# Cross-attention over 1601 keys: chunks of keys taken in pairs, with one value projection for two chunks

## The chip, the core and the metric

The kernel runs on one core of one Trainium2 chip. The metric is the device time of one execution in microseconds (us). Time before: 2998.97 us, the median of 3 runs (2998.92 to 2999.44).

The engines are named as in the profile: PE (TensorE, the matmuls), PEld (its weight loads), DVE (VectorE), ACT (ScalarE), POOL (GpSimd), SP (the queue that issues DMAs).

## What is computed

Six layers in a row on x, 16 x 64 x 256 (batch, queries, width), in fp32. The change touches the first and the fourth, two cross-attentions with 16 heads of 16 from the 64 queries to 1601 context rows:

```python
q = query @ Wq + bq;  k = key @ Wk + bk;  v = value @ Wv + bv      # per head: 64 x 16, 1601 x 16, 1601 x 16
attn = softmax((q @ k.T + relative) / sqrt(16))                    # layer 0: relative positions; layer 3: a mask of keys
x = x + (attn @ v (+ relative values)) @ Wo + bo
```

Between and after them stand a latent attention, a mixture of experts, a delta-rule layer and a gated MLP, which the change leaves alone.

## The kernel before

`cross_attention` (from L149) is called twice, once with `rel` (relative positions; "layer 0" below) and once with `mask` ("layer 1" below, the second cross-attention). It walks over the 16 batches b, two per loop turn (p = 0, 1). Each engine has a `body(bank, plan, i, p, flags)` with its own order of work, written out by hand, and engines meet only at semaphores. An engine takes its instructions strictly in this order.

One body does three things at once: it attends for batch b, prepares the keys and the score maxima of batch b + 1 ("ahead"), and finishes the output of batch b - 1 ("tail"). The first body (b = 0) has no tail and the last (b = 15) nothing ahead; the 14 between have all three.

The 1601 keys are 13 chunks (NCH) of 128, the last of 65. For each chunk c, PE does:

- the value projection: 2 matmuls of 256 columns on the whole 128 x 128 array, into bank `PJ[0]` (L726). As fp32 each is recorded as two. DVE copies the result from the bank into the buffer `V` (L537), which has 2 places;
- `scores(c)`: bf16 matmuls that subtract the row maximum (L688) and fp32 matmuls of q and k (L692), all on 32-row tiles of the array, four at a time, into banks 1 to 4. ACT takes the exponential of all four banks into a place of `PT` (L433); `scores(c + 1)` waits for it, since there is one set of score banks;
- `attend_values(c - 1)`: 16 matmuls of 64 columns (32 as recorded) on 32-column tiles of the array (L678), from V and PT, summed in bank 7.

Between these stand 16 units `maximum(u)`: bf16 scores of batch b + 1 for one of 4 key blocks and a quarter of the heads (L636, L640, in layer 0 also L645 for the first four units), into banks 5 and 6, on 32-row tiles. DVE reduces them (L525). There is one pair of banks for this, so `maximum(u)` on PE waits until DVE has read `maximum(u - 1)` (`max_read`). The tables EARLY and LATE (L278, L279) say after which chunk's value projection, or after which value product, a unit stands.

The tail of batch b - 1 also stands in this sequence: `denominators()` at c = 2 (L654: one matmul into bank 5, then on DVE a reciprocal and a product, L506 and L508) and `output()` at c = 5 (L663: the output projection into bank 6, then DVE adds it to X, L518). Banks 5 and 6 are those of the maxima, so both wait on the maxima already issued:

```python
if ahead:
    pe.wait_ge(max_read, UN * (b + 1) + U_DEN)     # U_DEN = 2: units 0 and 1 have been read
...
    pe.wait_ge(max_read, UN * (b + 1) + U_WO)      # U_WO = 6: units 0 to 5 have been read
```

In the order of before, unit 1 stands at the end of chunk 1, with chunk 2's projection, scores and a value product between it and `denominators()`; unit 5 stands after the projection of chunk 5, with the scores and a value product between it and `output()`. After the 13 chunks come, for batch b + 1, eight key projections (L584, 11 us), and at the start of the next body a transpose of the maxima (L721) that DVE turns into `nmb` (L530).

Of the kernel before, what the change touches and what calls it, by code (L numbers as in the profile page):

```python
# [13 lines left out]
B, S, D = 16, 64, 256  # L14
# [136 lines left out]
def cross_attention(nc, g, n, ctx_t, w, rel=None, mask=None):  # L151
# [5 lines left out]
    with nc.cleanup_on_exit(), ExitStack() as ctx:  # L157
        def sb(name, shape, dt=F32):
            return ctx.enter_context(nc.sbuf_tensor(tag + name, shape, dt))
# [22 lines left out]
        V = sb("V", [128, 2, H, 32])  # L182
        PT = sb("PT", [128, 3, H * S])
# [56 lines left out]
        class Schedule:  # L240
# [3 lines left out]
            def __init__(self, bank, ahead, attend, tail):  # L244
                self.D = bank.use(0) if rel and ahead else None
                self.K = [[bank.use(1 + gg) for gg in (0, 1)] for _ in range(NKB)] if ahead else None
                self.NM = bank.use(0) if attend else None
                self.V = [bank.use(0) for _ in range(NCH)] if attend else None
                self.DEN, self.WO = (bank.use(1), bank.use(2)) if tail else (None, None)
# [77 lines left out]
        def _(pool):  # L327
# [5 lines left out]
            def body(bank, plan, i, p, flags):  # L333
# [33 lines left out]
                if attend and rel:  # L367

                    pool.wait_ge(exp_done, NCH * b + 1)
                    if later(b):  # L370
                        pool.wait_ge(rv_done, b)
                    for j in range(RD):
                        pool.tensor_tensor(  # L373
                            Ej[:, j, :].rearrange("p (h q) -> p h q", h=H),
                            PT[:, 2, :].rearrange("p (h q) -> p h q", h=H),
                            kmask[:, j, None, :].to_broadcast([128, H, S]), ALU.mult).then_inc(e_done, 1)
# [7 lines left out]
        def _(act):  # L384
# [19 lines left out]
            def body(bank, plan, i, p, flags):  # L404
# [13 lines left out]
                if attend:  # L418
                    if mask:
                        act.wait_ge(kbs_done, b + 1)  # L420
                    for c in range(NCH):
                        slot = 2 if c == 0 else c % 2
# [26 lines left out]
        def _(dve):  # L449
# [23 lines left out]
            def body(bank, plan, i, p, flags):  # L473
# [58 lines left out]
                for c in range(NCH) if attend else ():  # L532
                    pb, use = plan.V[c]
# [5 lines left out]
                    if ahead and c in EARLY:  # L539
                        maximum(EARLY[c])  # L540
                    if ahead and c in LATE:
                        maximum(LATE[c])
# [27 lines left out]
        def _(pe):  # L570
# [38 lines left out]
            def body(bank, plan, i, p, flags):  # L609
# [56 lines left out]

                def attend_values(c):
                    pe.wait_ge(exp_done, NCH * b + c + 1)
                    pb, use = plan.V[c]
# [5 lines left out]
                    slot = 2 if c == 0 else c % 2  # L675
                    for h in range(H):
                        r = 32 * (h % 4)
                        last = pe.matmul(OT[r:r + 32, S * (h // 4):S * (h // 4) + S], V[0:CHK[c], c % 2, h, :],  # L678
# [38 lines left out]
                if attend:  # L717
# [5 lines left out]
                    for c in range(NCH):  # L723
                        pb = take(bank, plan.V[c])
                        for cc in range(KC):
                            last = pe.matmul(PJ[pb][0:CHK[c], 0:D], cT[:, p, cc, 128 * c:128 * c + CHK[c]],  # L726
                                             wv[:, cc, :], start=cc == 0, stop=cc == KC - 1)
                        last.then_inc(full[pb], 1)
                        if ahead and c in EARLY:
                            maximum(EARLY[c])  # L730
                        if c == 0:
                            pb, use = plan.NM
                            pe.wait_ge(free[pb], bank.value(pb, use))
                            if rel:
                                pe.wait_ge(dx_done, b + 1)
                        scores(c)
                        if c:
                            attend_values(c - 1)
                        if ahead and c in LATE:
                            maximum(LATE[c])  # L740
                        if tail and c == C_DEN:
                            denominators()
                        if tail and c == C_WO:
                            output()
# [1720 lines left out]
```

## Time and profile before

| | |
|---|---|
| median of 3 runs | 2998.97 us |
| the profiled execution's own time | 2999.0 us |
| its span, first to last instruction | 2996.8 us |
| PE busy | 2745.4 us (92%) |
| DVE busy | 1402.4 us (47%) |
| ACT busy | 1068.5 us (36%) |
| POOL busy | 478.0 us (16%) |
| mean granted TensorE clock, whole span | 0.963 of 2.4 GHz |

Times in the rows are microseconds from the start of the span unless marked ns. A matmul's record ends with a modelled tail, so busy sums of PE overlap; where a change of kind costs time is better read from the starts of the weight loads (PEld), which is how the rows below are used. In a timeline, neighbouring instructions of one kind are merged into a row with their count.

### The profile page before, as it was taken

To read this page: it belongs to the slowest core of one execution; us is meant where nothing else is said; L and a number is where in the kernel's file an instruction comes from. 1 tells how busy PE (TensorE), PEld (TensorE's weight loads), DVE (VectorE), ACT (ScalarE), POOL (GpSimd) and SP (SyncE) were. 2 spreads that over 40 slices of the span, in tenths; PEclk is the share of its full clock that TensorE was granted. 3 is DMA by queue.
4 is the path that set the end of the run, shared out by engine and by line. 5 is a ranking of instruction groups with operands and counts; after the bars stand their busy time and mean duration, and the time that the engine had idled before them with its cause. 6 is when DMAs were issued, how large, how long until landed. Compare 5 with 4: busy or idle time off the path is not lost. (4 is left out here: it accounts for less than half of the span.)

```text
span 2996.8 us, 95364 instructions
## 1 busy us (share of the span) xinstructions
PE 2745.4 (92%) x43444; PEld 1882.4 (63%) x43444; DVE 1402.4 (47%) x2425; ACT 1068.5 (36%) x1483; POOL 478.0 (16%) x406
## 2 busy tenths in 40 slices
PE   6999999999998789988999999999968999998798
PEld 3666666666666556655666666666646777777565
DVE  3443544544544821115454544545444555454378
ACT  2333333333332321123434344343434444444323
POOL 2424334234232000001000000000001112111000
PEclk8999999999998689999999999999979999999899
DMA  2110110111100011030111111111020000000100
GB/s 85 30 41 24 35 35 24 35 35 30 35 8 13 1 43 42 28 122 18 29 41 29 35 35 30 40 27 38 8 78 3 3 3 3 3 3 4 75 1 15
DMA packets 48631, 88.97 MB, mean 30 GB/s; under 512 B 8496, under 2 KB 43120, under 8 KB 46832
## 3 DMA queue, kind: packets, MB, share of 16 engines
q1 hardware_dynamic: 48240, 82.96, 9.1%
q8 instruction: 343, 5.62, 0.8%
q14 instruction: 48, 0.39, 0.0%
HBM read 81.89 MB, written 1.05 MB: 28 GB/s over the span
## 5 line engine op out<-in xcount | busy, mean ns | idle before, releaser
L525 DVE TENSOR_REDUCE x_mx<-banks 128x2 f32<-128x800 f32 (+1 forms) x512 | 506.9, 992 | 306.1 <-PE banks L640 217.0
L726 PE MATMUL banks<-x_wv,x_cT 128*128 128x256 f32 (+1 forms) x1664 | 465.9, 402 | 24.2 <-DVE x_nmb L530 21.1
L584 PE MATMUL banks<-x_cT,x_wk 128*128 128x400 f32 (+1 forms) x1024 | 362.9, 510 | 18.0 <-DMA x_cT<-in_ctx 18.0
L726 PEld LDWEIGHTS banks<-x_wv,x_cT 128*128 128x128 f32 (+1 forms) x1664 | 278.7, 186 | 145.4 <-issue 75.7
L433 ACT ACTIVATE x_PT<-banks 128x1024 f32<-128x1024 f32 (+1 forms) x208 | 212.8, 1023 | 430.0 <-PE banks L692 358.5
L433 ACT ACTIVATE x_PT<-banks,x_kbs 128x1024 f32<-128x1024 f32 (+1 forms) x208 | 231.5, 1113 | 376.7 <-PE banks L692 376.7
L584 PEld LDWEIGHTS banks<-x_cT,x_wk 128*128 128x128 f32 x1024 | 193.0, 192 | 163.6 <-issue 27.6
L692 PE MATMUL banks<-x_qbd,x_kT 32*128 32x128 f32 x6656 | 294.3, 273 | 0.0
L678 PE MATMUL banks<-x_PT,x_V 128*32 128x64 f32 x13312 | 272.1, 222 | 20.7 <-ACT x_PT L433 20.7
L692 PEld LDWEIGHTS banks<-x_qbd,x_kT 32*128 32x128 f32 x6656 | 253.2, 182 | 0.0
L678 PEld LDWEIGHTS banks<-x_PT,x_V 128*32 128x32 f32 x13312 | 204.9, 109 | 73.7 <-ACT x_PT L433 25.8
L389 ACT ACTIVATE x_kT<-banks,x_bk 128x400 f32<-128x400 f32 (+1 forms) x256 | 152.2, 595 | 255.2 <-PE banks L584 255.2
L365 POOL CAST x_kbf<-x_kT 128x800 bf16<-128x800 f32 (+1 forms) x128 | 110.3, 874 | 773.0 <-ACT x_kT L389 724.0
L537 DVE COPY x_V<-banks 128x256 f32<-128x256 f32 (+1 forms) x416 | 176.1, 423 | 122.5 <-PE banks L726 107.3
L640 PE MATMUL banks<-x_kbf,x_qbf 32*128 32x400 bf16 (+1 forms) x1024 | 173.1, 334 | 11.8 <-POOL x_kbf L365 7.4
L373 POOL TENSOR_TENSOR x_Ej<-x_PT,x_kmask 128x1024 f32<-128x1024 f32 x64 | 151.6, 2400 | 93.4 <-ACT x_PT L433 93.4
L530 DVE TENSOR_TENSOR x_nmb<-banks,x_pmask 128x256 bf16<-128x256 f32 x32 | 13.6, 424 | 308.2 <-PE banks L721 308.2
L688 PE MATMUL banks<-x_nmb,x_ones 32*128 32x256 bf16 (+1 forms) x1664 | 155.6, 277 | 1.8 <-ACT x_PT L433 1.8
L1840 PE MATMUL banks<-d_KQ,d_KB 64*64 64x64 f32 x3584 | 129.7, 221 | 8.2 <-ACT d_KB L1524 3.5
L1204 DVE SCALAR_TENSOR_TENSOR X<-banks,e_comb,X 128x256 f32<-128x256 f32 x72 | 34.8, 484 | 209.7 <-PE banks L1242 198.1
L1840 PEld LDWEIGHTS banks<-d_KQ,d_KB 64*64 64x64 f32 x3584 | 117.0, 133 | 22.1 <-issue 21.9
L1229 PE MATMUL banks<-XNT,e_wu 128*128 128x512 f32 x288 | 128.5, 600 | 0.4 <-DVE e_pr L1165 0.4
(321 smaller groups left out, 3776.3 us busy)
## 6 DMA issues: line engine op xcount, KB each, us to landing
x_cT<-in_ctx SPq DMA_DIRECT2D x96, 400.0 KB, 3.7
x_cT<-in_ctx SPq DMA_DIRECT2D x32, 401.0 KB, 3.6
e_wu<-in_mo_up SPq DMA_DIRECT2D x9, 512.0 KB, 3.6
e_wd<-in_mo_down SPq DMA_DIRECT2D x9, 512.0 KB, 4.4
x_mrow<-in_mask_row SPq DMA_DIRECT2D x1, 3202.0 KB, 11.1
t_w<-in_db_w SPq DMA_DIRECT2D x3, 1024.0 KB, 7.5
d_wqk<-in_db_qk SPq DMA_DIRECT2D x1, 2048.0 KB, 8.0
t_wgu<-in_fp_gu SPq DMA_DIRECT2D x1, 1536.0 KB, 10.4
```

The costliest lines, as they stand in the source:

```text
L373: pool.tensor_tensor(Ej[:, j, :].rearrange("p (h q) -> p h q", h=H), PT[:, 2, :].rearrange("p (h q) -> p h q", h=H), kmask[:, j, None, :]. ...
L389: act.activation(kT[:, 1 - p, gg, KB0[k]:KB0[k] + KBS[k]], PJ[pb][:, 0:KBS[k]], ACT.Identity, bias=bk[:, gg:gg + 1]).then_inc(free[pb], 1)
L433: act.activation(PT[0:CHK[c], slot, :].rearrange("p (r x) -> p r x", r=RT), g.PS[0:CHK[c], 1:1 + RT, 0:WS], ACT.Exp, scale=HD ** -0.5, bia ...
L525: dve.reduce_max(mx[:, H0[k]:H0[k] + 3:2, kb], g.PS[:, first:first + 2, 0:KBS[kb]], AXX).then_inc(max_read, 1)
L537: dve.tensor_copy(V[0:CHK[c], c % 2, :, 0:HD], PJ[pb][0:CHK[c], 0:D].rearrange("p (h d) -> p h d", h=H)).then_inc(free[pb], 1)
L584: last = pe.matmul(PJ[pb][:, 0:KBS[k]], wk[:, c, gg, :], cT[:, (p + 1) % 2, c, KB0[k]:KB0[k] + KBS[k]], start=c == 0, stop=c == KC - 1)
L640: last = pe.matmul(g.P[first + x][:, 0:KBS[kb]], qbf[rows(r), gg, :, :].rearrange("p i q -> p (i q)"), kbf[rows(r), gg, keys], start=not m ...
L678: last = pe.matmul(OT[r:r + 32, S * (h // 4):S * (h // 4) + S], V[0:CHK[c], c % 2, h, :], PT[0:CHK[c], slot, S * h:S * h + S], start=c == ...
L688: pe.matmul(SC[r][0:CHK[c], 0:WS], ones[rows(r), 0:CHK[c]], nmb[rows(r), :, :].rearrange("p j q -> p (j q)"), start=True, stop=False, skip ...
L692: last = pe.matmul(SC[r][0:CHK[c], HPT * S * gg:HPT * S * gg + HPT * S], kT[rows(r), p, gg, 128 * c:128 * c + CHK[c]], qbd[rows(r), p, gg, ...
L726: last = pe.matmul(PJ[pb][0:CHK[c], 0:D], cT[:, p, cc, 128 * c:128 * c + CHK[c]], wv[:, cc, :], start=cc == 0, stop=cc == KC - 1)
L1840: last = pe.matmul(out, lhs(E[e], hp), rhs(E[e], hp), start=k > 0 or start, stop=True, skip_group_check=True)
```

## The change

In both cross-attentions the chunks are walked in pairs. One value projection covers two chunks: 4 matmuls of 256 columns into the two halves of bank `PJ[0]`, one semaphore, and one DVE copy of 512 elements per partition. V gets 4 places instead of 2, PT 4 instead of 3. The order on PE for a pair (c, c + 1), c even, becomes: scores(c), a maximum (SCORED), projection of c + 2 and c + 3, a maximum (VALUED), scores(c + 1), attend_values(c - 1), a maximum (BETWEEN), attend_values(c). `denominators()` stands right behind the SCORED maximum of c = 2, which is unit 1, and `output()` right behind the VALUED maximum of c = 4, which is unit 5 (C_WO goes from 5 to 4). DVE's order follows. The waits inside `maximum`, `denominators` and `output` are unchanged. The diff, cut to its core:

```diff
-        V = sb("V", [128, 2, H, 32])
-        PT = sb("PT", [128, 3, H * S])
+        V = sb("V", [128, 4, H, 32])
+        PT = sb("PT", [128, 4, H * S])
...
-        EARLY = {4: 3, 5: 5, 6: 6, 8: 9, 10: 12, 12: 15}
-        LATE = {0: 0, 1: 1, 3: 2, 4: 4, 6: 7, 7: 8, 8: 10, 9: 11, 10: 13, 11: 14}
+        SCORED = {2: 1, 4: 4, 6: 7, 8: 10, 10: 13}
+        VALUED = {2: 2, 4: 5, 6: 8, 8: 11, 10: 14}
+        BETWEEN = {0: 0, 2: 3, 4: 6, 6: 9, 8: 12, 10: 15}
         C_DEN, U_DEN = 2, 2
-        C_WO, U_WO = 5, 6
+        C_WO, U_WO = 4, 6
...
-                        elif c >= 3:
-                            act.wait_ge(av_done, NCH * b + c - 1)
+                        elif c >= 4:
+                            act.wait_ge(av_done, NCH * b + c - 2)
...
+                def values(c):
+                    n2 = min(2, NCH - c)
+                    pb, use = plan.V[c // 2]
                     dve.wait_ge(full[pb], bank.value(pb, use))
-                    if later(b) or c >= 2:
-                        dve.wait_ge(av_done, NCH * b + (c - 1 if c >= 2 else 0))
-                    dve.tensor_copy(V[0:CHK[c], c % 2, :, 0:HD],
-                                    PJ[pb][0:CHK[c], 0:D].rearrange("p (h d) -> p h d", h=H)).then_inc(free[pb], 1)
+                    if later(b) or c >= 4:
+                        dve.wait_ge(av_done, NCH * b + (c - 2 if c >= 4 else 0))
+                    dve.tensor_copy(V[0:CHK[c], c % 4:c % 4 + n2, :, 0:HD],
+                                    PJ[pb][0:CHK[c], 0:D * n2].rearrange("p (a h d) -> p a h d", a=n2, h=H)).then_inc(free[pb], 1)
+                if attend:
+                    values(0)
+                for c in range(0, NCH, 2) if attend else ():
+                    if ahead and c in SCORED:
+                        maximum(SCORED[c])
                     if tail and c == C_DEN:
                         denominators()
+                    if ahead and c in VALUED:
+                        maximum(VALUED[c])
                     if tail and c == C_WO:
                         add_output()
+                    if c + 2 < NCH:
+                        values(c + 2)
+                    if ahead and c in BETWEEN:
+                        maximum(BETWEEN[c])
...
+                    project_values(0)
+                    for c in range(0, NCH, 2):
                         scores(c)
+                        if ahead and c in SCORED:
+                            maximum(SCORED[c])
+                        if tail and c == C_DEN:
+                            denominators()
+                        if c + 2 < NCH:
+                            project_values(c + 2)
+                        if ahead and c in VALUED:
+                            maximum(VALUED[c])
+                        if tail and c == C_WO:
+                            output()
+                        if c + 1 < NCH:
+                            scores(c + 1)
                         if c:
                             attend_values(c - 1)
+                        if ahead and c in BETWEEN:
+                            maximum(BETWEEN[c])
+                        if c + 1 < NCH:
+                            attend_values(c)
                     attend_values(NCH - 1)
```

## Rows read from the trace of the kernel before

**Rows 1.** Stretches inside layers 0 and 1: busy us (instructions) by engine, granted clock, DMA.

```profile
core 0: us, PE busy (x) PEld busy (x) DVE busy (x) ACT busy (x) POOL busy (x), PEclk, DMA share, GB/s
126.00:850.00 724.00, 705.59 (x11573) 472.43 (x11574) 333.77 (x497) 241.59 (x288) 250.72 (x171) 1.00 0.12 32
...
1430.00:2165.00 735.00, 711.28 (x11934) 458.60 (x11936) 356.44 (x520) 297.32 (x322) 47.06 (x55) 1.00 0.11 31
```

**Rows 2.** Waits of PE in the stretch 1430 to 2165 (layer 1).

```profile
PE banks L678 <- ACT x_PT L433: 9.7, 14, 0.7
PE banks L726 <- DVE x_nmb L530: 8.2, 15, 0.5
```

**Rows 3.** Timeline of weight loads: first projection of two neighbouring batches, layers 0 and 1.

```profile
291.35 0.73 PEld L726 LDWEIGHTS banks<-x_wv,x_cT 128*128 128x128 f32 x4 [0.82 <-DVE x_nmb L530]
...
346.52 0.73 PEld L726 LDWEIGHTS banks<-x_wv,x_cT 128*128 128x128 f32 x4 [0.81 <-DVE x_nmb L530]
...
1488.40 0.73 PEld L726 LDWEIGHTS banks<-x_wv,x_cT 128*128 128x128 f32 x4 [0.82 <-DVE x_nmb L530]
...
1540.63 0.73 PEld L726 LDWEIGHTS banks<-x_wv,x_cT 128*128 128x128 f32 x4 [0.81 <-DVE x_nmb L530]
```

**Rows 4.** Timeline of weight loads, layer 1, about chunks 8 and 9.

```profile
1512.61 0.73 PEld L726 LDWEIGHTS banks<-x_wv,x_cT 128*128 128x128 f32 x4 [0.33 <-issue]
1513.77 0.09 PEld L636 LDWEIGHTS banks<-x_mb,x_ones 32*128 32x128 bf16 x2 [0.43 <-DVE x_mx L525]
...
1514.77 0.49 PEld L678 LDWEIGHTS banks<-x_PT,x_V 128*32 128x32 f32 x32
1515.37 0.09 PEld L636 LDWEIGHTS banks<-x_mb,x_ones 32*128 32x128 bf16 x2
...
1515.82 0.73 PEld L726 LDWEIGHTS banks<-x_wv,x_cT 128*128 128x128 f32 x4 [0.33 <-issue]
1516.88 0.10 PEld L688 LDWEIGHTS banks<-x_nmb,x_ones 32*128 32x128 bf16 x4 [0.33 <-issue]
...
1517.55 0.49 PEld L678 LDWEIGHTS banks<-x_PT,x_V 128*32 128x32 f32 x32
```

**Rows 5.** Timeline of weight loads, layer 1: denominators, then the projection of chunk 3.

```profile
1495.54 0.30 PEld L654 LDWEIGHTS banks<-x_oT,x_selden 128*128 128x128 f32 x2
...
1497.03 0.10 PEld L688 LDWEIGHTS banks<-x_nmb,x_ones 32*128 32x128 bf16 x4 [0.33 <-issue]
```

**Rows 6.** Timeline of weight loads, layer 0: a maximum before scores, another before a projection.

```profile
318.31 0.09 PEld L640 LDWEIGHTS banks<-x_kbf,x_qbf 32*128 32x128 bf16 x2 [0.43 <-DVE x_mx L525]
...
319.14 0.49 PEld L678 LDWEIGHTS banks<-x_PT,x_V 128*32 128x32 f32 x32
319.75 0.09 PEld L640 LDWEIGHTS banks<-x_kbf,x_qbf 32*128 32x128 bf16 x2
320.02 0.73 PEld L726 LDWEIGHTS banks<-x_wv,x_cT 128*128 128x128 f32 x4 [0.18 <-issue]
```

**Rows 7.** Timeline of DVE: a reduction in layer 0, the reciprocal and a reduction in layer 1.

```profile
318.70 0.99 DVE L525 TENSOR_REDUCE x_mx<-banks 128x2 f32<-128x800 f32 x1
...
1496.28 1.76 DVE L506 RECIPROCAL x_rec<-banks 128x256 f32<-128x256 f32 x1 [1.46 <-PE banks L654]
...
1514.33 0.99 DVE L525 TENSOR_REDUCE x_mx<-banks 128x2 f32<-128x800 f32 x1
```

**Rows 8.** Groups by line and shape: busy us, mean ns of one | idle before.

```profile
L525 DVE TENSOR_REDUCE x_mx<-banks 128x2 f32<-128x800 f32 x384 | 379.8, 992 | 189.3 <-PE banks L640 183.1 <-issue 1.3
...
L433 ACT ACTIVATE x_PT<-banks,x_kbs 128x1024 f32<-128x1024 f32 x192 | 213.8, 1113 | 344.9 <-PE banks L692 344.9
L433 ACT ACTIVATE x_PT<-banks 128x1024 f32<-128x1024 f32 x192 | 196.5, 1023 | 401.9 <-PE banks L692 330.4 <-PE banks L699 71.5
...
L537 DVE COPY x_V<-banks 128x256 f32<-128x256 f32 x384 | 162.6, 423 | 118.5 <-PE banks L726 103.6
```

**Rows 9.** Timeline of ACT, layer 1: the exponential of the scores issued at 1516.88.

```profile
1517.75 1.11 ACT L433 ACTIVATE x_PT<-banks,x_kbs 128x1024 f32<-128x1024 f32 x1 [1.66 <-PE banks L692]
```

More of the change, by code:

```diff
@@ L247, in __init__ @@
                 self.NM = bank.use(0) if attend else None
-                self.V = [bank.use(0) for _ in range(NCH)] if attend else None
+                self.V = [bank.use(0) for _ in range(0, NCH, 2)] if attend else None
                 self.DEN, self.WO = (bank.use(1), bank.use(2)) if tail else (None, None)
@@ L421, in body @@
                     for c in range(NCH):
-                        slot = 2 if c == 0 else c % 2
+                        slot = 3 if c == 0 else c % 3
                         if c == 0:
@@ L531, in body @@
                                       pmask[:, :, None].to_broadcast([128, NPR, 128]), ALU.mult).then_inc(free[pb], 1)
-                for c in range(NCH) if attend else ():
-                    pb, use = plan.V[c]
+                def values(c):
+                    n2 = min(2, NCH - c)
+                    pb, use = plan.V[c // 2]
                     dve.wait_ge(full[pb], bank.value(pb, use))
-                    if later(b) or c >= 2:
-                        dve.wait_ge(av_done, NCH * b + (c - 1 if c >= 2 else 0))
-                    dve.tensor_copy(V[0:CHK[c], c % 2, :, 0:HD],
-                                    PJ[pb][0:CHK[c], 0:D].rearrange("p (h d) -> p h d", h=H)).then_inc(free[pb], 1)
[L539 to L542, printed above, removed]
+                    if later(b) or c >= 4:
[7 more added lines that the diff above has]
+                        maximum(SCORED[c])
                     if tail and c == C_DEN:
                         denominators()
+                    if ahead and c in VALUED:
+                        maximum(VALUED[c])
                     if tail and c == C_WO:
                         add_output()
+                    if c + 2 < NCH:
+                        values(c + 2)
+                    if ahead and c in BETWEEN:
+                        maximum(BETWEEN[c])
                 if ahead:
@@ L665, in output, with project_values @@
                     last.then_inc(full[pb], 1)
+                def project_values(c):
+                    pb = take(bank, plan.V[c // 2])
+                    for k in range(min(2, NCH - c)):
+                        for cc in range(KC):
+                            last = pe.matmul(PJ[pb][0:CHK[c + k], D * k:D * k + D], cT[:, p, cc, 128 * (c + k):128 * (c + k) + CHK[c + k]],
+                                             wv[:, cc, :], start=cc == 0, stop=cc == KC - 1)
+                    last.then_inc(full[pb], 1)
                 def attend_values(c):
                     pe.wait_ge(exp_done, NCH * b + c + 1)
-                    pb, use = plan.V[c]
+                    pb, use = plan.V[c // 2]
                     pe.wait_ge(free[pb], bank.value(pb, use))
@@ L674, in attend_values @@
                         pe.wait_ge(bias_out, 1)
-                    slot = 2 if c == 0 else c % 2
+                    slot = 3 if c == 0 else c % 3
                     for h in range(H):
                         r = 32 * (h % 4)
-                        last = pe.matmul(OT[r:r + 32, S * (h // 4):S * (h // 4) + S], V[0:CHK[c], c % 2, h, :],
+                        last = pe.matmul(OT[r:r + 32, S * (h // 4):S * (h // 4) + S], V[0:CHK[c], c % 4, h, :],
                                          PT[0:CHK[c], slot, S * h:S * h + S], start=c == 0 and h < 4,
@@ L722, in body @@
                     last.then_inc(full[pb], 1)
[L723 to L735, printed above, removed]
-                        scores(c)
+                    project_values(0)
+                    pb, use = plan.NM
+                    pe.wait_ge(free[pb], bank.value(pb, use))
+                    if rel:
+                        pe.wait_ge(dx_done, b + 1)
+                    for c in range(0, NCH, 2):
+                        scores(c)
+                        if ahead and c in SCORED:
[10 more added lines that the diff above has]
+                            scores(c + 1)
                         if c:
                             attend_values(c - 1)
[L739 to L744, printed above, removed]
+                        if ahead and c in BETWEEN:
+                            maximum(BETWEEN[c])
+                        if c + 1 < NCH:
+                            attend_values(c)
                     attend_values(NCH - 1)
```

2 lines of the change are left out of this document (1 added, 1 removed).

## The prediction

> **What bounds the kernel now.** I read first the busy table by stretch. Inside both cross-attentions PE is busy 97% of the time (705.59 of 724 us, 711.28 of 735) and no other engine half; the granted clock is 1.00 throughout, the 2.4 GHz level, and the DMAs are busy 12% [rows 1]. So only PE's sequence counts: what it issues, and what makes it wait. A batch takes 55.17 us in layer 0 and 52.23 us in layer 1, from one first projection to the next [rows 3]. PE's waits come to under 1.5 us of that [rows 2]; but those rows count idle time behind modelled matmul tails, and short waits vanish in them. So I went on to the starts of the weight loads. There every group of PE has a length from its first weight load to that of the next group [rows 4]: projection 1.06 us (1515.82 to 1516.88), scores 0.67 (to 1517.55), value product 0.60 (1514.77 to 1515.37; 0.58 in most places), maximum 0.45 (to 1515.82). In layer 0 a maximum is 0.27 (319.75 to 320.02) [rows 6].
>
> **What a change of kind costs.** Denominators and the projection behind them are both whole-array matmuls of 256 columns, six records together, and take 1.49 us [rows 5], against 1.06 for four: 0.215 per record, so four records cost 0.86 and the projection's entry and exit 0.20. A maximum of 0.45 and scores of 0.67 take 1.00 when they touch (1513.77 to 1514.77) [rows 4], 0.11 less; in layer 0 0.83 [rows 6]. These are what joining two groups of one kind saves. The trace shows no two projections side by side; the bounds are 0 and 0.20, and I take 0.20, the nearest row being the denominators with a projection.
>
> **What is removed.** The 13 projection groups become 7, six joins: 1.18 us a batch. In layer 0 chunk 2's projection also joins the relative-bias matmuls behind the first scores, 0.20 more. Maxima and scores touch more often (22 groups of 32-row kind become 19): 0.33. The value products join nothing: BETWEEN puts a maximum between the two of a pair, so "one run" is not what happens while a batch lies ahead. In layer 0 the first four maxima end in whole-array matmuls, which now meet a projection once instead of three times: 0.35 given back. Four of the new joins are spoiled by waits (below), 0.05 each. Net about -1.2 us in layer 0, -1.3 in layer 1. Waits also go. A maximum behind a projection waits 0.10 (1512.61 to 1513.77 is 1.16, not 1.06) [rows 4]; four such go, and with them the wait of chunk 4's projection for its bank, 0.2: -0.65 us.
>
> By the Trainium skill, TensorEngine Tiling (Key Properties), changing the tiling mode drains the engine. The trace agrees: 0.20 and 0.11 us per change in the joins above.
>
> **The cycle of a maximum.** Weights at 1513.77 [rows 4], reduction from 1514.33 for 0.99 [rows 7, 8], next maximum at 1515.37 [rows 4]: 1.60 us in layer 1. In layer 0 318.31, 318.70 [rows 6, 7], 319.75: 1.44. Nothing that waits on `max_read` can start sooner.
>
> **What is added: two long waits.** `denominators()` needs units 0 and 1 read, and now stands right behind unit 1. PE goes on 1.60 us after unit 1 began, of which 0.39 is the unit's own work: 1.2 us idle. In layer 0 the extra bias matmuls of units 0 to 3 lengthen both: 1.25. `output()` needs units 0 to 5 and stands right behind unit 5: again 1.2. Before, scores and a value product (1.25 us) lay between in the second case, more in the first; now nothing does, and everything later on PE is queued behind. Nothing hides them. That is 2.4 us a batch in both layers. Unit 2 must also wait until the reciprocal (1.76 us) [rows 7] has freed bank 5; it stands 0.54 + 1.92 us behind the start of the denominators: 0.2 more.
>
> **Shorter new waits.** (a) Scores(2) follow scores(1) with one maximum and one value product between. The exponential begins 0.87 us after its scores (1516.88 to 1517.75) [rows 4, 9], takes 1.11 or 1.02 [rows 8], and PE follows 0.06 later: 2.05 or 1.96 us. PE's own work there is 1.00 + 0.58 = 1.58 in layer 1: a wait of 0.47; in layer 0, with the bias matmuls, 0.22. For later pairs there are two value products between, 2.2 us and more: no wait. (b) The copy of V of two chunks. Reductions of 800 elements take 992 ns and copies of 256 take 423 [rows 8], so 1.046 ns an element: 0.69 us for 512. The bounds are 0.60 (the fixed part smaller) and 0.75. The copy waits for the value product just before the BETWEEN maximum, so it runs from 0.10 to 0.75 after that maximum's weights, its reduction from 0.78 to 1.77, and the SCORED maximum of the next pair cannot begin before 1.83. PE is there after 0.45 + 0.58 + 0.67 = 1.70 in layer 1 and 1.52 in layer 0: 0.13 and 0.31. In layer 0 this holds in three pairs (0.95), in layer 1 in four, one of them 0.18 (0.57); unit 1 is caught by (a) already, and unit 4 in layer 0 comes late enough. (c) In layer 1 chunk 2's projection waits 0.18 for the doubled copy of the first pair. The last wait of a batch, value product 12 for its exponential, stays.
>
> By the Trainium skill, VectorE: DVE Perf Modes (The TRN2 errata), a copy from PSUM costs 120 cycles plus one per element: 0.66 us for 512, an estimate. By it the result would be 4 us lower.
>
> **The sum.** Layer 0, per batch: 1.25 + 1.19 + 0.19 + 0.22 + 0.95 = 3.80, less 0.65 of waits and 1.2 of joins: +1.9. Layer 1: 1.19 + 1.19 + 0.19 + 0.47 + 0.57 + 0.18 = 3.79, less 0.65 and 1.3: +1.8. As a test of the method I laid out a whole batch, group by group and engine by engine, with these durations: the order of before comes out at 55.1 and 52.4 us, against 55.17 and 52.23 measured, and the new order at 57.0 and 54.2. 14 batches of each layer have everything: 14 x 3.7 = +51.8 us. The first batch has no denominators and no output, so only the gains and the small waits: -0.9 and -0.7. The last has no maxima; its value products do touch, but then scores wait for the exponential of the scores just before: -0.7 and +0.2. Together +49.7, rounded to 49. ACT, POOL and the loads of the context stay hidden (ACT has 1.6 us free per chunk, [rows 9]). Against the profiled execution's 2999.0 us (span 2996.8 and 2.2 around it), which equals the median of 2998.97, that gives 3048 us.
>
> **Rivals.**
>
> *The joins win* (faster). If every wait on `max_read` were covered, only joins and removed waits were left: -1.85 us in layer 0 and -1.95 in layer 1, times 14, and -2 for the edges, so about -55: 2944 us. For it speaks that PE takes weight loads ahead of running matmuls, so that a wait may cost less than the distance of starts suggests. It needs the waits cut by half to become faster: 3.8 us a batch would have to be under 1.9. Against it: the order in the code is plain, and the cycle of 1.60 us is seen at every second maximum, where PE does wait its 0.1. Taken alone, the Trainium skill's rule on draining (above) would give this case. Chance 0.07.
>
> *The two long waits are half as dear* (near no change). If the reduction of units 1 and 5 ran while something else of PE did, say because the tail's waits were met earlier than I read, 1.2 us a batch would go: 28 x 1.2 = 34 us less, 3014 us; with cheaper copies on top it could reach 3000. Chance 0.07.
>
> *Waits breed waits* (slower than forecast). DVE falls behind after the reciprocal and each maximum then finds its pair of banks late. Each further 0.3 us in five places a batch is 1.5 x 28 = 42 us: 3090. Against it: DVE is busy less than half of the time [rows 1], and the layout by engine already has its queue. Chance 0.08.
>
> *The clock.* The new waits of 1.2 us could drop the granted clock inside the stages. In [rows 1] it stays at 1.00 with the waits there are (0.8 at the start of each batch [rows 3]). If it fell to the 1.2 GHz level for a tenth of the 1510 us of both layers, that would cost some 75 us: 3120. Chance 0.03.
>
> **How the numbers follow.** The forecast, two waits of 1.2 us a batch and small ones, has 0.75. Its own range: the copy's bounds move the sum by -12 and +7, the joins (six a batch at 0.15 to 0.20) by up to +8, the small waits by -8 to +6: 3028 to 3066. Stretched to take in part of the milder and the dearer case: 3022 to 3068. A measurement of this kernel can tell about 0.2% (6 us) from no change. Faster than 2993: 0.08. Within: 0.03. Slower than 3005: 0.89.
>
> **What would show it.** In the profile after, DVE rows in the weight loads of L654 and L663 (in the new numbering) with some 1.2 us of idle time, 28 each; projections as eight records at 0.215 us each; V copies of 512 elements at 0.69 us; 57.0 and 54.2 us between first projections; granted clock 1.00. The forecast fails if PE shows no wait before the denominators and the output, or if two projections side by side take over 2.0 us, or if exponentials hold scores in every pair and not only at scores(2).

## The result

The changed kernel takes 3076.05 us, the median of 4 runs (3074.35 to 3078.87), against 2999.2 for the kernel before on the same chips: a ratio of 1.0253, 95% interval 1.0237 to 1.0268. It is 77 us slower. The forecast was 3048 us, 49 slower, with a range up to 3068: the direction was right, and a good third of the loss was missing.

The profile after, first the page's busy line and then the same two stretches as in [rows 1]:

```profile
PE 2715.8 (88%) x43444; PEld 1891.2 (62%) x43444; DVE 1392.9 (45%) x2233; ACT 1069.6 (35%) x1483; POOL 480.1 (16%) x406
```

```profile
126.00:850.00 724.00, 651.56 (x10856) 447.48 (x10854) 327.75 (x394) 226.74 (x269) 239.71 (x163) 1.00 0.11 30
1430.00:2165.00 735.00, 673.86 (x11453) 444.98 (x11454) 326.61 (x420) 286.36 (x309) 44.59 (x52) 1.00 0.12 32
```

PE is busy 90% and 92% of the stages instead of 97%, at the same granted clock of 1.00: it waits more. Time from one first projection to the next, as in [rows 3]:

```profile
359.99 1.59 PEld L681 LDWEIGHTS banks<-x_wv,x_cT 128*128 128x128 f32 x8 [0.82 <-DVE x_nmb L531]
...
418.60 1.59 PEld L681 LDWEIGHTS banks<-x_wv,x_cT 128*128 128x128 f32 x8 [0.81 <-DVE x_nmb L531]
```

```profile
1532.47 1.59 PEld L681 LDWEIGHTS banks<-x_wv,x_cT 128*128 128x128 f32 x8 [0.82 <-DVE x_nmb L531]
...
1586.76 1.59 PEld L681 LDWEIGHTS banks<-x_wv,x_cT 128*128 128x128 f32 x8 [0.81 <-DVE x_nmb L531]
```

That is 58.61 us a batch in layer 0 (before 55.17, forecast 57.0) and 54.29 in layer 1 (before 52.23, forecast 54.2). Times 14: 48 + 29 = 77 us. (The interval behind batch 14 is some 12 us shorter, since the key projections stand at the start of the next body, for the batch behind it, and the last body has none; it grows by the same 3.45 and 2.06 us.) Layer 1 is nearly as forecast; in layer 0 the forecast misses 1.6 us a batch.

The two long waits, in weight loads of layer 1 after, and then the reductions of units 1 and 5 on the vector engine:

```profile
1539.61 0.10 PEld L646 LDWEIGHTS banks<-x_mb,x_ones 32*128 32x128 bf16 x2
1539.72 0.10 PEld L650 LDWEIGHTS banks<-x_kbf,x_qbf 32*128 32x128 bf16 x2
1541.33 0.30 PEld L664 LDWEIGHTS banks<-x_oT,x_selden 128*128 128x128 f32 x2 [1.51 <-issue]
1541.66 1.70 PEld L681 LDWEIGHTS banks<-x_wv,x_cT 128*128 128x128 f32 x8
...
1549.78 0.09 PEld L646 LDWEIGHTS banks<-x_mb,x_ones 32*128 32x128 bf16 x2 [0.33 <-issue]
...
1551.40 1.49 PEld L673 LDWEIGHTS banks<-x_wo,x_oN 128*64 128x64 f32 x8 [1.51 <-issue]
```

```profile
1540.27 0.99 DVE L526 TENSOR_REDUCE x_mx<-banks 128x2 f32<-128x802 f32 x1 [0.99 <-PE banks L650]
...
1550.34 0.99 DVE L526 TENSOR_REDUCE x_mx<-banks 128x2 f32<-128x800 f32 x1 [1.38 <-PE banks L650]
```

From the weights of unit 1 to those of the denominators are 1.72 us, from those of unit 5 to those of the output projection 1.62, with a maximum of about 0.4 as the only work in between. Both follow the end of the reduction that the code makes them wait for by 0.07 us (1541.26 to 1541.33, 1551.33 to 1551.40). The profile puts the wait down to "issue" and not to the vector engine, where the forecast had looked for it.

And the place that the forecast did not see, layer 0 after. PE's loads, then the vector engine, then GpSimd, at the same time:

```profile
373.69 0.54 PEld L710 LDWEIGHTS banks<-x_qbd,x_kT 32*128 32x128 f32 x16
374.35 0.49 PEld L696 LDWEIGHTS banks<-x_PT,x_V 128*32 128x32 f32 x32
376.38 0.09 PEld L650 LDWEIGHTS banks<-x_kbf,x_qbf 32*128 32x128 bf16 x2 [1.54 <-DVE x_mx L526]
```

```profile
371.26 1.76 DVE L507 RECIPROCAL x_rec<-banks 128x256 f32<-128x256 f32 x1 [0.81 <-PE banks L664]
373.05 2.37 DVE L509 TENSOR_TENSOR x_oN<-x_oT,x_rec 128x256 f32<-128x256 f32 x1
375.35 0.98 DVE L526 TENSOR_REDUCE x_mx<-banks 128x2 f32<-128x802 f32 x1
```

```profile
365.86 9.28 POOL L374 TENSOR_TENSOR x_Ej<-x_PT,x_kmask 128x1024 f32<-128x1024 f32 x4 [5.13 <-ACT x_PT L434]
375.08 0.94 POOL L342 COPY x_qs<-x_qT 128x256 f32<-128x256 f32 x2
```

The product of 256 elements takes 2.37 us and ends just after GpSimd's four multiplications end (375.14). The reduction of unit 2 stands behind it on the vector engine, and PE waits 1.54 us for that before unit 3. In the kernel before, the same product took 0.48:

```profile
301.36 1.76 DVE L506 RECIPROCAL x_rec<-banks 128x256 f32<-128x256 f32 x1 [1.46 <-PE banks L654]
303.15 0.48 DVE L508 TENSOR_TENSOR x_oN<-x_oT,x_rec 128x256 f32<-128x256 f32 x1
```

```profile
296.36 9.48 POOL L373 TENSOR_TENSOR x_Ej<-x_PT,x_kmask 128x1024 f32<-128x1024 f32 x4 [4.27 <-ACT x_PT L433]
```

```profile
L373 POOL TENSOR_TENSOR x_Ej<-x_PT,x_kmask x4: 2358/2360/2542, 296.4 to 303.3; 128x1024 f32<-128x1024 f32 x4
```

(minimum, median and maximum in ns, then the first and the last start). It began at 303.15, just ahead of the start of the fourth of GpSimd's multiplications, at 303.3. That fourth one took 2.54 us there and the other three 2.36: here it was the product that came first. So the theory to test has three parts: two waits behind maxima, a product that GpSimd holds, and short waits that eat what the pairs save. Its rival: the rhythm of pairs itself is slow, and any wait taken away comes back at the next maximum.

### The profile page after: what moved, and what is told of

Same layout as the page of the kernel before. It is cut to its first block and busy times, and to the rows that moved or that the text cites. A ratio compares the mean times of both kernels' runs of the same rounds, so it can differ in the third digit from the quotient of the medians.

```text
span 3072.6 us, 94948 instructions
## 1 busy us (share of the span) xinstructions
PE 2715.8 (88%) x43444; PEld 1891.2 (62%) x43444; DVE 1392.9 (45%) x2233; ACT 1069.6 (35%) x1483; POOL 480.1 (16%) x406
## 5 line engine op out<-in xcount | busy, mean ns | idle before, releaser
L681 PE MATMUL banks<-x_wv,x_cT 128*128 128x256 f32 (+1 forms) x1664 | 417.5, 393 | 22.8 <-DVE x_nmb L531 21.1
L681 PEld LDWEIGHTS banks<-x_wv,x_cT 128*128 128x128 f32 (+1 forms) x1664 | 296.9, 188 | 104.2 <-issue 31.1
L710 PE MATMUL banks<-x_qbd,x_kT 32*128 32x128 f32 x6656 | 282.5, 271 | 0.0
L539 DVE COPY x_V<-banks 128x512 f32<-128x512 f32 (+1 forms) x224 | 146.0, 652 | 241.7 <-PE banks L681 163.0
L710 PEld LDWEIGHTS banks<-x_qbd,x_kT 32*128 32x128 f32 x6656 | 245.0, 182 | 0.0
L706 PE MATMUL banks<-x_nmb,x_ones 32*128 32x256 bf16 (+1 forms) x1664 | 143.6, 278 | 10.7 <-ACT x_PT L434 9.4
## 6 DMA issues: line engine op xcount, KB each, us to landing
x_mrow<-in_mask_row SPq DMA_DIRECT2D x1, 3202.0 KB, 11.1
```

What stands on the lines that cost most here:

```text
L539: dve.tensor_copy(V[0:CHK[c], c % 4:c % 4 + n2, :, 0:HD], PJ[pb][0:CHK[c], 0:D * n2].rearrange("p (a h d) -> p a h d", a=n2, h=H)).then_in ...
L681: last = pe.matmul(PJ[pb][0:CHK[c + k], D * k:D * k + D], cT[:, p, cc, 128 * (c + k):128 * (c + k) + CHK[c + k]], wv[:, cc, :], start=cc = ...
L706: pe.matmul(SC[r][0:CHK[c], 0:WS], ones[rows(r), 0:CHK[c]], nmb[rows(r), :, :].rearrange("p j q -> p (j q)"), start=True, stop=False, skip ...
L710: last = pe.matmul(SC[r][0:CHK[c], HPT * S * gg:HPT * S * gg + HPT * S], kT[rows(r), p, gg, 128 * c:128 * c + CHK[c]], qbd[rows(r), p, gg, ...
```

## The experiments

Each kernel is the changed one with one edit, unless said otherwise. "Batch" is the usual time between first projections, layer 0 / layer 1; ratios are to the kernel before on the same chip. A line `...` in a diff stands for lines left out.

**The output projection behind a value product.**

```diff
-                        if tail and c == C_WO:
-                            output()
                         if c + 1 < NCH:
                             scores(c + 1)
                         if c:
                             attend_values(c - 1)
+                        if tail and c == C_WO:
+                            output()
```

> The changed kernel with the output projection moved from right behind unit 5 to behind the value product of chunk 3, so that scores and a value product lie between unit 5 and it. Theory A (the wait behind unit 5 is a pure loss of about 1.2 us a batch in both layers): it goes, and unit 6, now right behind the output, waits 0.6 us for the addition to X; net -0.8 in both layers, 28 batches, 3076 - 23 = about 3053 us; 57.8 us a batch in layer 0 and 53.5 in layer 1. Theory B (the rhythm of the pairs sets the time and a wait taken away comes back at the next maximum): 3070 to 3080 us, batches still 58.6 and 54.3.

Measured: 3047.49 us, ratio 1.0159 (1.0142 to 1.0176); batch 57.58 / 53.38. The wait is gone and did not come back in full. What takes its place is the one that was expected, unit 6 behind the addition to X:

```profile
1541.03 1.49 PEld L673 LDWEIGHTS banks<-x_wo,x_oN 128*64 128x64 f32 x8
1543.48 0.09 PEld L646 LDWEIGHTS banks<-x_mb,x_ones 32*128 32x128 bf16 x2 [0.97 <-DVE X L519]
```

2.45 us for a group of 1.87: 0.6 waited. In all -29 us, a little more than the 23 expected. The batches of theory B, 58.6 and 54.3, are not seen: it falls for this wait.

**Units 0 and 1 one place earlier**, so that a value product and scores lie between unit 1 and the denominators.

```diff
-        SCORED = {2: 1, 4: 4, 6: 7, 8: 10, 10: 13}
+        SCORED = {0: 0, 4: 4, 6: 7, 8: 10, 10: 13}
-        BETWEEN = {0: 0, 2: 3, 4: 6, 6: 9, 8: 12, 10: 15}
+        BETWEEN = {0: 1, 2: 3, 4: 6, 6: 9, 8: 12, 10: 15}
```

> The changed kernel with unit 0 behind the scores of chunk 0 and unit 1 in unit 0's old place, so that a value product and scores lie between unit 1 and the denominators. Theory A: the 1.2 us wait before the denominators goes in both layers. In layer 0 the product behind the reciprocal starts earlier, at another point of GpSimd's four multiplications, and if it is those that hold it (2.37 us instead of 0.48) it takes 1.2 to 1.6 us now. Batches 56.5 and 52.9 us, 3076 - 45 = about 3031 us. Theory B: the wait comes back later, 3065 to 3080 us. If GpSimd has nothing to do with the product's length, it stays at 2.4 us.

Measured: 3021.22 us, ratio 1.0079 (1.0062 to 1.0096); batch 56.30 / 52.94. -55 us, the largest gain of one edit, and in layer 0 (-2.3) more than in layer 1 (-1.35), since the held product shortens too: it now begins nearer to the end of one of GpSimd's multiplications. So the 55 us hold part of two causes. GpSimd's multiplications of the same batch stand below the product:

```profile
246.56 1.76 DVE L507 RECIPROCAL x_rec<-banks 128x256 f32<-128x256 f32 x1 [1.04 <-PE banks L664]
248.35 1.06 DVE L509 TENSOR_TENSOR x_oN<-x_oT,x_rec 128x256 f32<-128x256 f32 x1
```

```profile
242.16 9.47 POOL L374 TENSOR_TENSOR x_Ej<-x_PT,x_kmask 128x1024 f32<-128x1024 f32 x4 [5.13 <-ACT x_PT L434]
```

1.06 us, shorter than the 1.2 to 1.6 expected, but neither 0.48 nor 2.37.

**GpSimd's multiplications cut to a quarter.** The relative values of 12 of the 16 heads are left out (their part of Ej is set to zero once).

```diff
...
-                            Ej[:, j, :].rearrange("p (h q) -> p h q", h=H),
-                            PT[:, 3, :].rearrange("p (h q) -> p h q", h=H),
-                            kmask[:, j, None, :].to_broadcast([128, H, S]), ALU.mult).then_inc(e_done, 1)
+                            Ej[:, j, 0:256].rearrange("p (h q) -> p h q", h=4),
+                            PT[:, 3, 0:256].rearrange("p (h q) -> p h q", h=4),
+                            kmask[:, j, None, :].to_broadcast([128, 4, S]), ALU.mult).then_inc(e_done, 1)
```

> The changed kernel with GpSimd's four multiplications of exponentials and key masks in layer 0 cut to the first quarter of the columns (4 of 16 heads; the rest of Ej stays zero, so the relative values of the other heads are left out). Nothing else differs. If GpSimd's running multiplication holds the product of the normalised output on the vector engine (L509), the product takes 0.42 to 0.48 us again, the wait of 1.4 us before unit 3 is gone and layer 0 takes 57.0 us a batch: 3076 - 22 = about 3054 us. If the product is long for another reason, 2.37 us and 3076 us stay. Layer 1 stays at 54.3 in both.

Measured: 3056.35 us, ratio 1.0188 (1.0171 to 1.0205); batch 57.25 / 54.31. All 32 products take the same time again:

```profile
L512 DVE TENSOR_TENSOR x_oN<-x_oT,x_rec x32: 424/425/427, 135.9 to 2251.4; 128x256 f32<-128x256 f32 x32
```

(minimum, median and maximum in ns). -20 us, all of it in layer 0, against 22 expected. The product begins as far behind the start of the multiplications as in the changed kernel (7.19 us); only they are shorter. That GpSimd's running multiplication holds the product is shown, and with it most of what the forecast missed: layer 0 comes to 57.25, where it had 57.0.

**The kernel before, with the product 0.4 us later.** A copy out of the bank is put in front of the reciprocal.

```diff
...
+                    dve.tensor_copy(rec2[:, :], PJ[pb][:, 0:4 * S])
                     dve.reciprocal(rec[:, :], PJ[pb][:, 0:4 * S]).then_inc(free[pb], 1)
```

> The kernel before with a copy of 0.42 us out of the bank put in front of the reciprocal on the vector engine, nothing else. If the product escaped GpSimd only because it began in the gap between the third and the fourth multiplication (303.15 us against 303.30), it now begins 0.25 us into the fourth and takes about 2.1 us instead of 0.48 in layer 0; unit 2 and chunk 4's projection then wait some 1.5 us longer: 14 to 15 x 1.5 to 2 us = 3020 to 3030 us, with layer 1 only up to 0.4 us a batch slower. If the collision is not the cause, the product stays at 0.48 us and the kernel at 2999 to 3011 us.

Measured: 3056.42 us, ratio 1.0191 (1.0174 to 1.0208); batch 57.4 to 60.3 / 52.56. The product is held as in the changed kernel (GpSimd's multiplications below it):

```profile
192.49 0.42 DVE L507 COPY x_rec<-banks 128x256 f32<-128x256 f32 x1 [1.46 <-PE banks L656]
192.83 1.75 DVE L508 RECIPROCAL x_rec<-banks 128x256 f32<-128x256 f32 x1
194.61 2.45 DVE L510 TENSOR_TENSOR x_oN<-x_oT,x_rec 128x256 f32<-128x256 f32 x1
```

```profile
187.48 9.30 POOL L374 TENSOR_TENSOR x_Ej<-x_PT,x_kmask 128x1024 f32<-128x1024 f32 x4 [4.26 <-ACT x_PT L434]
```

So the kernel before stood on an edge: 0.4 us of added work in layer 0 cost 2.3 us a batch at least, 32 us in 14 batches. The total is 57 us instead of the expected 20 to 30, because a second thing came with it. PE's wait for the copy behind the product is 2.3 us here, and in layer 0 the granted clock falls:

```profile
197.45 1.35 PEld L728 LDWEIGHTS banks<-x_wv,x_cT 128*128 128x128 f32 x4 [2.32 <-DVE x_V L539]
```

```profile
195.00:205.00 10.00, 7.85 (x92) 5.13 (x93) 6.19 (x8) 1.16 (x2) 2.66 (x3) 0.66 0.16 44
205.00:215.00 10.00, 9.91 (x194) 6.73 (x190) 5.64 (x9) 3.07 (x3) 0.00 (x0) 1.00 0.16 43
```

A mean of 0.66 in ten microseconds means that PE ran part of them at the 1.2 GHz level, and the same load group took 1.35 us instead of 0.73. The 11 batches whose mean granted clock is 0.97 or 0.94 take 58.8 to 60.3 us, the two at 1.00 take 57.4; the same wait of 2.3 us stands in all of them. With batch 14, whose interval is the short one, the excess over 57.4 comes to about 24 us.

**The doubled copy behind the reduction.**

```diff
-                    if c + 2 < NCH:
-                        values(c + 2)
                     if ahead and c in BETWEEN:
                         maximum(BETWEEN[c])
+                    if c + 2 < NCH:
+                        values(c + 2)
```

> The changed kernel with the copy of V of two chunks moved behind the reduction of the BETWEEN maximum on the vector engine. The forecast put 0.31 us in three pairs of layer 0 and 0.13 in four of layer 1 on that copy standing ahead of the reduction. If that is right the maximum no longer waits, but the copy ends 1 us later, and the next projection of two chunks, which needs the bank, waits 0.5 us (layer 0) and 0.3 (layer 1) instead: 59.4 and 54.8 us a batch, 3076 + 19 = about 3095 us. If the copy in front is the only cost there (the bank is free in time): 58.6 - 0.9 and 54.3 - 0.5 us a batch, 3056 us.

Measured: 3070.44 us, ratio 1.0241 (1.0224 to 1.0259); batch about 58.6 / 53.83. Both expectations missed. Layer 1 gains 0.47, nearly the 0.5 of the second case; layer 0 gains nothing. Moved behind, the copy makes the next projection wait for the bank (0.07 to 0.15 us in layer 1, some 0.3 in layer 0), and where the maxima are short, in layer 0, that takes back all that is gained before the next maximum. 0.5 and 0.3 us for that wait were too much. In layer 1 the four waits that came come to 0.5 us, so those that went with the copy in front were about 1.0 us a batch and not the 0.57 of the forecast.

**Both long waits away, and the product moved.** The first two edits, and on the vector engine the product behind unit 2's reduction, in a function of its own.

```diff
...
                     if tail and c == C_DEN:
                         denominators()
                     if ahead and c in VALUED:
                         maximum(VALUED[c])
+                    if tail and c == C_DEN:
+                        product()
```

> The changed kernel with both moves together (output projection behind the value product of chunk 3, units 0 and 1 one place earlier) and the product of the normalised output behind the reduction of unit 2, so that no maximum waits for it. Theory A (two waits and the held product are the whole loss, and their costs add up): 55.9 us a batch in layer 0 and 52.4 in layer 1, near the 55.2 and 52.2 of before: 3000 to 3012 us. That it is no faster than before although PE has six changes of kind less is then due to the shorter waits that stay (scores(2) for the exponential, a maximum behind the copy of two chunks, unit 6 for the addition). Theory B (the pairs as such are slow): 3020 us or more.

Measured: 3009.22 us, ratio 1.0036 (1.0024 to 1.0049); batch 56.44 / 52.04. 67 of the 77 us are back: layer 1 at the level of before, layer 0 still 1.3 above. In layer 1 the gains of the first two edits add up (0.92 + 1.36 us a batch, which gives 52.0). In layer 0 they would give 55.3, an estimate from the two runs, and 56.44 is measured, so there the third edit did harm. Moved, the product begins 7.83 us behind the start of the multiplications, in the middle of the fourth, takes 1.74 us, and now unit 3's reduction stands behind it; PE waits 1.39 us before unit 4:

```profile
308.32 1.74 DVE L512 TENSOR_TENSOR x_oN<-x_oT,x_rec 128x256 f32<-128x256 f32 x1
...
310.59 0.98 DVE L529 TENSOR_REDUCE x_mx<-banks 128x2 f32<-128x802 f32 x1
```

```profile
311.69 0.12 PEld L656 LDWEIGHTS banks<-x_kbf,x_qbf 32*128 32x128 bf16 x2 [1.39 <-issue]
```

**A new order for the pairs.** The pairs, doubled projections, copies and buffers are kept. Both orders are written as lists (V projection, S scores, A value product, M maximum, D denominators, P product, W output):

```diff
+        ORDER = ("V0 N S0 M0 V2 M1 S1 A0 M2 S2 D V4 S3 M3 A1 A2 S4 M4 "
+                 "V6 M5 S5 A3 M6 A4 S6 M7 V8 W S7 M8 A5 A6 S8 M9 V10 M10 "
+                 "S9 A7 M11 A8 S10 M12 V12 S11 M13 A9 A10 M14 S12 A11 M15 A12 ").split()
+        ORDER_DVE = ("V0 M0 V2 M1 M2 D M3 V4 M4 P M5 V6 M6 M7 W M8 V8 M9 "
+                     "M10 V10 M11 M12 M13 V12 M14 M15 ").split()
...
+        U_DEN = 3
+        U_WO = 8
```

> The pairs, the doubled projection, the doubled copy and the four buffers are kept; only the order is written anew, as one list for PE and one for the vector engine, so that 1.4 us or more of PE's work lies between two maxima wherever it can, the denominators stand two groups behind the last maximum they need (three units read), the output projection behind a projection (eight units read), and the product behind unit 4's reduction. Theory A (what a pair saves in changes of kind is real, and only waits on single buffers ate it): with the durations of the rows the order comes to 53.8 us a batch in layer 0 and 50.6 in layer 1, 14 x (-1.4 - 1.6) - 4 = 46 us less than the kernel before: about 2953 us. Theory B (the joins give nothing on the chip): 2990 to 3010 us.

Measured: 2948.65 us, ratio 0.9838 (0.9821 to 0.9854), 1.6% faster than the kernel before; batch 53.80 / 50.53, where 53.8 and 50.6 were expected. In layer 1:

```profile
1477.44 0.09 PEld L642 LDWEIGHTS banks<-x_mb,x_ones 32*128 32x128 bf16 x2 [0.25 <-DVE x_mx L531]
...
1477.88 1.59 PEld L677 LDWEIGHTS banks<-x_wv,x_cT 128*128 128x128 f32 x8 [0.33 <-issue]
1479.80 1.49 PEld L669 LDWEIGHTS banks<-x_wo,x_oN 128*64 128x64 f32 x8 [0.33 <-issue]
1481.67 0.10 PEld L702 LDWEIGHTS banks<-x_nmb,x_ones 32*128 32x128 bf16 x4 [0.39 <-issue]
```

The output projection follows the projection of V without a wait (1477.88 to 1479.80 is 1.92, the doubled projection alone). In layer 0 the product now stands behind unit 4's reduction, 11.1 us behind the start of GpSimd's multiplications, which end after 9.3, and takes 0.41 us in all full batches:

```profile
300.59 0.41 DVE L514 TENSOR_TENSOR x_oN<-x_oT,x_rec 128x256 f32<-128x256 f32 x1
```

The total of theory B (2990 to 3010 us) is not seen. But this run changes the places of the maxima, the denominators, the product and the output too, so by itself it does not say how much the pairs give.

**The halves apart.** The same order, but the second chunk's two matmuls of each doubled projection stand behind the next scores (v):

```diff
-        ORDER = ("V0 N S0 M0 V2 M1 S1 A0 M2 S2 D V4 S3 M3 A1 A2 S4 M4 "
+        ORDER = ("V0 N S0 v0 M0 V2 M1 S1 v2 A0 M2 S2 D V4 S3 v4 M3 A1 "
...
```

> The kernel of the new order with the two halves of each doubled projection set apart on PE: the second chunk's two matmuls stand behind the next scores instead of behind the first chunk's. Work, copies and waits stay. If joining two projections saves 0.20 us (entry and exit of the whole-array kind), five to six joins a batch are undone: up to 11 x 0.2 x 15 = 33 us slower than the new order, 2949 + 33 = 2982 us, somewhat less where the added time covers a wait for a maximum: 2970 to 2982. If a join gives nothing, the kernel stays at 2945 to 2953 us.

Measured: 3049.47 us, ratio 1.0189 (1.0167 to 1.0211); batch 56.78 / 53.70. That is 101 us more than with the halves joined, three times what was expected. Some 14 of them are the clock: five batches of layer 1 take 55.3 us and three of layer 0 58.5 to 58.8, each at a mean granted clock of 0.97 where the others have 1.00. The trace has a wait of 1.26 us before unit 2, and another before the denominators:

```profile
1577.56 0.49 PEld L697 LDWEIGHTS banks<-x_PT,x_V 128*32 128x32 f32 x32 [0.33 <-issue]
1579.31 0.09 PEld L643 LDWEIGHTS banks<-x_mb,x_ones 32*128 32x128 bf16 x2 [1.26 <-DVE x_mx L532]
...
1580.93 0.30 PEld L661 LDWEIGHTS banks<-x_oT,x_selden 128*128 128x128 f32 x2 [0.74 <-issue]
```

On the vector engine the copy of the pair, which now had to wait for the late half, stood ahead of unit 1's reduction:

```profile
1577.66 0.69 DVE L545 COPY x_V<-banks 128x512 f32<-128x512 f32 x1 [2.38 <-PE banks L678]
1578.27 0.98 DVE L532 TENSOR_REDUCE x_mx<-banks 128x2 f32<-128x802 f32 x1
```

One more kernel mends only that:

```diff
-        ORDER_DVE = ("V0 M0 V2 M1 M2 D M3 V4 M4 P M5 V6 M6 M7 W M8 V8 M9 "
+        ORDER_DVE = ("V0 M0 M1 V2 M2 D M3 V4 M4 P M5 V6 M6 M7 W M8 V8 M9 "
...
```

> The kernel with the halves apart once more, with one thing mended: on the vector engine unit 1's reduction stands ahead of the copy of chunks 2 and 3. In the kernel before it the second half of that pair ended only after scores(1), so the copy held back the reduction that unit 2 and the denominators wait for (1.17 us before unit 2, 0.7 before the denominators in the trace). If that was what made the halves cost 3 us a batch instead of 1.2, 1.3 to 1.9 of them go: layer 1 at 52.0 to 52.5 us a batch, layer 0 at 55.1 to 55.6, in all 3000 to 3015 us, and what is left over the new order (50.5 and 53.8) is five or six joins of projections at 0.20 and three of scores and maxima at 0.11. If the order on the vector engine does not matter, 3045 to 3052 us stay.

Measured: 3002.33 us, ratio 1.0032 (1.0022 to 1.0042); batch 55.62 / 52.53. 47 us came from the place of one copy on the vector engine, the batches at 0.97 included: here all of both layers behind the first stay at 1.00. The halves apart now cost 1.8 and 2.0 us a batch; five or six joins of projections at 0.20 and three of scores and maxima at 0.11 make 1.3 to 1.5 of them. What the rest is was not followed. So the joins are worth about 40 us in this order, an estimate from these sizes, and with them undone the new order stands at the kernel before (ratio 1.0032). The new order with single projections and single copies was not run.

## Why the prediction fell short

**The direction and the two long waits: right.** The forecast had 1.2 us behind units 1 and 5 in each of 28 batches; the loads of the denominators and the output stand 1.72 and 1.62 us behind those of the maximum, whose own part is 0.4. Moving the output away gives 29 us, with 0.6 us a batch coming back before unit 6; moving the denominators away gives 55, in layer 0 with a part of the held product.

**Layer 1: nearly right.** 54.2 was forecast, 54.29 measured. The added time is less close than that: the layout had put the batch of before at 52.4 instead of 52.23, so the sum took +1.8 us a batch where 2.06 are measured. The wait of scores(2) and the maximum behind the doubled copy are where they were put. The first is 0.40 us for a forecast of 0.47; the four waits behind the doubled copy are about 1.0 us a batch (read from the loads, and from the run with the copy moved) where the sum had 0.57, and 0.2 for the joins that they spoil. The copy of 512 elements takes 690 ns, as forecast (0.69). The estimate from the Trainium skill's page VectorE: DVE Perf Modes (The TRN2 errata) was 0.66; the measurement decides for 0.69.

**Layer 0: the step "ACT, POOL and the loads of the context stay hidden" failed.** The sum for layer 0 took over the product behind the reciprocal at its length of before, without naming it among the prices, and looked at GpSimd only as a chain whose results come in time. It moved the product to another point of GpSimd's four multiplications, and never asked what the two engines do to each other there. Measured: 2.37 us instead of 0.48, and 1.54 us of PE waiting before unit 3. 1.5 x 14 = 21 us, most of the 28 missing; the run with short multiplications gives 20. The kernel before hid this: its products in 14 batches of layer 0 took 0.47 to 0.49. Counted from the start of the first multiplication, the product of layer 0 begins and ends here:

| kernel | begins | takes | ends |
|---|---|---|---|
| units 0 and 1 earlier | 6.19 | 1.06 | 7.25 |
| before | 6.79 | 0.48 | 7.27 |
| before, with the copy | 7.13 | 2.45 | 9.58 |
| changed | 7.19 | 2.37 | 9.56 |
| product moved | 7.83 | 1.74 | 9.57 |

Whenever it begins, it ends at one of two times, 0.2 to 0.3 us behind the end of the third or of the fourth multiplication. So it waits for the running one to end, and that holds for the kernel before too, which only waited least. The change moved the product by 0.4 us, and the edge lies between 6.79 and 7.13: a margin of at most 0.34 us. That the product of before was short was luck in its timing, and the forecast leaned on it.

The Trainium skill states the rule on the page SBUF — State Buffer, in Who interferes with whom: a vector instruction with both inputs in SBUF contends with a GpSimd instruction that reads SBUF, whoever is first keeps the way for its whole instruction, and reductions do not contend. The trace agrees: the product (two inputs in SBUF) is held until a multiplication ends, while the reductions out of the banks during the same multiplications keep their 0.99 us; and where the product came first, in the kernel before, the fourth multiplication took 2.54 us instead of 2.36.

**The joins: right in size.** A doubled projection takes 1.92 us where two single ones take 2.12; the forecast took the upper of its bounds. That they were more than eaten by waits was the forecast too; the new order and the two runs with the halves apart show them as a gain once the waits are spread.

**The rest of the difference** is small. Of the 28 us missing 22 are layer 0's steady batches (3.44 us a batch for a forecast of 1.9) and 4 layer 1's (2.06 for 1.8). The first batches saved 0.5 and 1.8 us where 0.9 and 0.7 were forecast. Some batches take 0.3 to 0.5 us more, for which no cause was looked for, and one of layer 1 takes 1.5 us more, 55.79: there the granted clock fell right behind the wait before the denominators, and the doubled projection took 3.6 us instead of 1.9:

```profile
1976.45 0.34 PEld L664 LDWEIGHTS banks<-x_oT,x_selden 128*128 128x128 f32 x2 [1.51 <-issue]
1976.88 3.29 PEld L681 LDWEIGHTS banks<-x_wv,x_cT 128*128 128x128 f32 x8
```

```profile
1976.00:1980.00 4.00, 3.52 (x9) 2.83 (x10) 2.56 (x3) 0.20 (x1) 0.00 (x0) 0.58 0.00 0
```

Two slips of the working changed little: the upper terms of the range (+7, +8, +6) add to 3069 and not 3066, and the denominators add 0.43 us to a projection (1.49 less 1.06), not 0.54; from their start to unit 2 are 2.55 us, which is 0.43 + 1.92 and the 0.20 of waiting that the forecast had. The range was too narrow because its low and high ends came from the sizes of terms that were in the sum; a term that was not in it had no place.

**The rivals.** "The joins win" did not occur in this order of work; the new order comes near its 2944 us, with 2948.65, but by other places for the waits and not by waits that cost less. "Half as dear" did not occur: 1.72 and 1.62 us. "Waits breed waits" is nearest to what happened: a late reduction after the reciprocal. But its mechanism was a queue on a vector engine that is simply late, and here it is one instruction held by another engine. The clock stayed at 1.00 as the mean of both stages, as the forecast took it, but the rival on it came true in one batch of 28, for 1.5 us.

## What to carry to other kernels

When an order of work is rewritten, look at each wait on a single buffer (here one pair of banks, with 1.44 to 1.60 us from one use to the next) and put the next user at least that far away, on every engine's list: the same pairs cost 77 us in one order and gained 48 in another. When an instruction moves in time, ask also what other engines are doing at its new time; the vector product here, which reads two operands from SBUF, took the rest of the running GpSimd multiplication and 0.3 us more. A moved instruction whose length before was suspiciously short for its surroundings deserves a second look, since it may have met the other engine's boundary by luck. And moving it a little is not enough: 0.6 us later it was held again and did its harm one unit further on; behind the last multiplication it was free.

## What was not expected of the hardware

- A vector product of 256 elements (0.42 us alone) took 1.06, 1.74, 2.37 or 2.45 us, depending only on when it began within GpSimd's multiplications of 2.36 us: it always ended 0.2 to 0.3 us behind the end of one of them.
- In the kernel before with the added copy, a PE wait of 2.3 us stood in each full batch of layer 0. In 12 of 14 the granted clock then fell (0.66 over the ten microseconds around one of them), in two it stayed at 1.00. In the changed kernel one of 28 waits before the denominators, of 1.3 us, went with a fall (0.58 over the four microseconds behind it), and with the halves apart eight full batches had one. The same wait did and did not bring a fall, and what decides was not tried.
